# First batch of a cross-attention kernel on one core: the order of W_v·W_t, hnT's split, b_v's sums and z's first half

## The chip, the cores and the metric

The kernel runs on one core of a Trainium2 chip. The metric is the device time of one execution in microseconds (us); the median of several executions is compared.

## The reference

```python
B, C, N = (8, 256, 1024)          # x and ctx are [B, C, N], float32
def _L0_xattn_ref(x, y, w_qk, w_v, b_v, w_t, b_t):
    x_q = einsum('oc,bcn->bno', w_qk, y)
    x_k = einsum('oc,bcn->bon', w_qk, x)
    x_v = einsum('oc,bcn->bon', w_v, x) + b_v[None, :, None]
    energy = einsum('bnc,bcm->bnm', x_q, x_k)
    attention = softmax(energy, axis=-1)
    attention = attention / (1e-07 + attention.sum(axis=1, keepdims=True))
    x_r = einsum('bcn,bnm->bcm', x_v, attention)
    x_r = relu(einsum('oc,bcn->bon', w_t, x - x_r) + b_t[None, :, None])
    return x + x_r
```

The arrays that arrive hold 32 batches of this shape.

## The kernel before, in words

There is one stage ahead of everything (the set-up) and then 32 batches, of which the first is written out with orders of its own. Matmuls that need accuracy are made in three passes: each operand is split in a rounded part (hi) and a remainder (lo), and hi·hi, hi·lo and lo·hi are added up in PSUM. A "low part" is a remainder that is made by a subtraction on VectorE or GpSimd after ScalarE has made the rounded one.

The energy is y^T·G·x with G = W_qk^T·W_qk. G x is made first (four blocks of 128x512, each in a PSUM bank of its own: bank_c, bank_b, bank_a, bank_e), and then y^T·(G x) with seven products P1 to P7 of sums of blocks in place of eight. The sums of G x's blocks (T1, T2N, T4, T3) are made in the tile `ev` (also called t_raw), their parts go to gx_hi and gx_lo; the sums of y's blocks are in y_raw, y_hi and y_lo. z = x^T·(−W_v·W_t product) replaces V and the last projection: it needs hnT, the negated product of W_v and W_t, split in hnT_hi and hnT_lo.

There is no planner. Each engine has a queue of its own in the order in which the code is written, and semaphores hold an instruction until its inputs are there. An instruction that waits holds all that is behind it on its engine. The start of the first batch, in queue order:

- SyncE issues the loads: W_qk, two pieces of x, three pieces of y, W_t (L180), W_v (L181), b_v, b_t (L183, L184). The semaphore weights_in counts W_t and W_v.
- TensorE: warm-up on zeros (L869), G (L873), G·x's hi and lo·hi passes (L881, 16 matmuls of 512 columns), the pass with x's low parts (L886, 8 matmuls; each of the four blocks then counts g_done up), the product of W_v and W_t (L892, 8 matmuls of 256 columns), P1 (helper line L673, 3 matmuls), b_v's sums (L786, 8 matmuls of one column), z's first half (L736, 24 matmuls of 256 columns), P5, P6, P2, P7, P3, P4 (L673, 3 matmuls each), z's second half.
- ScalarE: the negated copy and the rounded parts of G x's blocks (L290, L291, L295, L297), y's rounded parts (L284), the rounded parts of the T sums (t_high, L303, two instructions), copies of P1's bank (L314).
- VectorE: G's split, x's low part, three sums of y, then gx_parts(0): low part of B11 (L441), T1 (L460), T2N (L464), the split of hnT (L451, L452), low part of B22 (L443), T4 (L471), low part of B21 (L443), and after it the low parts of T1 and T2N (L641, which counts t_lo_first), then bias (L644), neg_bias (L645) and eps_wb (L646).
- GpSimd: y_lo's first piece (L244), a sum of y (L246), T3 (L218, waits for T2N), y_low(0, 0) (L213), the low parts of T4 and T3 (t_low, L223), y_low for three further tiles (L213).

P1 waits for T1 (it overwrites its bank) and the low part of B11. z's first half waits for both parts of hnT. P5 waits for y_low(0, 0), for the low parts of G x's blocks and for t_lo_first, and P7 for GpSimd's t_low. ScalarE's copy of P1's bank waits for t_lo_first too, and P6 for this copy.

Of the kernel before, what the change touches and what calls it, by code (L numbers as in the profile page):

```python
# [16 lines left out]
DMA = 16  # L17
# [16 lines left out]
def xattn_kernel(nc: bass.Bass, x: bass.AP, y: bass.AP, w_qk: bass.AP, w_v: bass.AP, b_v: bass.AP,  # L34
                 w_t_T: bass.AP, b_t: bass.AP, out: bass.AP):
    B, C, N = x.shape
    KT = C // P
# [12 lines left out]
    with ctx:  # L50
# [3 lines left out]
        def sem(name):  # L54
            return ctx.enter_context(nc.semaphore(name))
# [36 lines left out]
        wv_sb = res[:, 0, KT * C:2 * KT * C].rearrange("p (k c) -> p k c", k=KT)  # L92
        wtT_sb = res[:, 1, 0:KT * C].rearrange("p (k c) -> p k c", k=KT)

        pv = ctx.enter_context(nc.psum_tensor("pv", [P, KT, N], FP32))
# [6 lines left out]
        wqk_in, weights_in, y_in = sem("wqk_in"), sem("weights_in"), sem("y_in")  # L102
# [3 lines left out]
        setup_mm, setup_dve = sem("setup_mm"), sem("setup_dve")  # L106
# [15 lines left out]
        gx_lo_done, t_made = sem("gx_lo_done"), sem("t_made")  # L122
# [305 lines left out]
        def _(dve):  # L428
            setup_steps = [0]

            def setup(ins):

                setup_steps[0] += 1
                ins.then_inc(setup_dve, 1)
                dve.wait_ge(setup_dve, setup_steps[0])

            def b_low(b, k, of, src, sign):
                dve.wait_ge(gx_hi_done, 3 * b + k + 1)
                hi = gx_hi[:, of, :].bitcast(FP32)
                if sign > 0:  # L440
                    nc.vector.tensor_tensor(gx_lo[:, of, :], src, hi, ALU.subtract).then_inc(gx_lo_done, 1)  # L441
                else:
                    nc.vector.scalar_tensor_tensor(out=gx_lo[:, of, :], in0=src, scalar=-1.0, in1=hi, op0=ALU.mult,  # L443
                                                   op1=ALU.subtract).then_inc(gx_lo_done, 1)
# [4 lines left out]
            def split_hnT():  # L449
                dve.wait_ge(setup_mm, KT + 1)  # L450
                setup(nc.vector.tensor_scalar(hnT_hi[:, :, :], h_ps, -1.0, None, ALU.mult))  # L451
                setup(nc.vector.scalar_tensor_tensor(out=hnT_lo[:, :, :], in0=h_ps, scalar=-1.0,  # L452
                                                     in1=hnT_hi[:, :, :].bitcast(FP32), op0=ALU.mult,
                                                     op1=ALU.subtract))

            def gx_parts(b, first=False):
                b_low(b, 0, B_11, row_b[:, left], 1)
                dve.wait_ge(neg_b11_made, b + 1)
                dve.wait_ge(g_done, 4 * b + 2)
                nc.vector.tensor_tensor(t_raw[:, T_1, :], row_b[:, right], neg_b11[:, :],  # L460
                                        ALU.add).then_inc(t_made, 1)
                dve.wait_ge(t_made, 3 * b + 1)
                dve.wait_ge(gx_hi_done, 3 * b + 2)
                nc.vector.tensor_tensor(t_raw[:, T_2N, :], t_raw[:, T_1, :], row_a[:, left],  # L464
                                        ALU.subtract).then_inc(t_made, 1)
                if first:
                    split_hnT()
                b_low(b, 1, B_N22, row_a[:, left], -1)
                dve.wait_ge(t_made, 3 * b + 2)
                dve.wait_ge(gx_hi_done, 3 * b + 3)  # L470
                nc.vector.scalar_tensor_tensor(out=t_raw[:, T_4, :], in0=row_a[:, right], scalar=-1.0,  # L471
                                               in1=t_raw[:, T_2N, :], op0=ALU.mult,
                                               op1=ALU.subtract).then_inc(t_made, 1)
                b_low(b, 2, B_N21, row_a[:, right], -1)
# [161 lines left out]
            nc.vector.tensor_tensor(y_raw[:, 6, :], y_raw[:, 0, :], y_raw[:, 1, :], ALU.add).then_inc(setup_y, 1)  # L636
            dve.wait_ge(setup_y, 1)
            nc.vector.tensor_tensor(y_raw[:, 5, :], y_raw[:, 4, :], y_raw[:, 1, :], ALU.add).then_inc(setup_y, 1)
            gx_parts(0, first=True)
            dve.wait_ge(t_hi_done, 1)  # L640
            nc.vector.tensor_tensor(gx_lo[:, 3:5, :], t_raw[:, 0:2, :], gx_hi[:, 3:5, :].bitcast(FP32),  # L641
                                    ALU.subtract).then_inc(t_lo_first, 1)
# [21 lines left out]
        def _(pe):  # L664
# [3 lines left out]
            def rows_of(tile):  # L668
                return slice(tile * P, (tile + 1) * P)

            def product(dst, t, ya, gb, start):
                for n, (a, g) in enumerate(((y_hi, gx_hi), (y_hi, gx_lo), (y_lo, gx_hi))):
                    last = nc.tensor.matmul(dst, a[:, ya, rows_of(t)], g[:, gb, :], start=start and n == 0,  # L673
                                            stop=n == 2, skip_group_check=not start)
                return last

            def p1(b, t, first=False):
                if first:
                    pe.wait_ge(a_lo_done, 1)
                else:  # L680
                    pe.wait_ge(y_lo_done, NP * b + t + 1)
                if t == 0:
                    pe.wait_ge(gx_lo_done, 3 * b + 1)
                    if not first:
                        pe.wait_ge(z_lo_done, 2 * b + 1)
                else:
                    pe.wait_ge(max_done, NT * b + 2 * t)
                product(bank_b, t, Y_A11, B_11, True).then_inc(b_done, 1)
# [42 lines left out]
            def z_half(par, h, first=False):  # L731
                dst = pv[:, h, :] if first else (row_b, row_a)[h][:, :]
                for i in range(NP):
                    for kt in range(KT):
                        for n, (v, w) in enumerate(((x_hi, hnT_hi), (x_hi, hnT_lo), (x_lo, hnT_hi))):
                            last = nc.tensor.matmul(dst[:, i * C:(i + 1) * C], v[par][:, kt, rows_of(h * NP + i)],  # L736
                                                    w[:, kt, :], start=(kt == 0 and n == 0),
                                                    stop=(kt == KT - 1 and n == 2))
                last.then_inc(z_done, 1)
# [38 lines left out]
                    last.then_inc(pv_done, 1)  # L778

            def very_first_pair():  # L780
                pe.wait_ge(t_made, 1)
                p1(0, 0, first=True)
                pe.wait_ge(bias_in, 2 * DMA)
                for mt in range(KT):
                    for kt in range(KT):
                        last = nc.tensor.matmul(pv[:, 1, mt:mt + 1], wtT_sb[:, kt, rows_of(mt)], bv_sb[:, kt:kt + 1],  # L786
                                                start=(kt == 0), stop=(kt == KT - 1))
                last.then_inc(setup_mm, 1)
                pe.wait_ge(setup_dve, 2)
                z_half(0, 0, first=True)  # L790
                pe.wait_ge(gx_lo_done, 3)
                pe.wait_ge(y_lo_done, 1)
                p5(0, 0, first=True)
                p6(0, 0, first=True)
                p2(0, 0)
                p7(0, 0)
                p3(0, 0).then_inc(row_a_done, 1)
                p4(0, 0)
                pe.wait_ge(setup_dve, 5)
                z_half(0, 1, first=True)  # L800
# [70 lines left out]
            for ct in range(KT):  # L871
                for kt in range(KT):
                    last = nc.tensor.matmul(pv[:, 0, ct * BANK:ct * BANK + C], wqk_sb[:, kt, rows_of(ct)],  # L873
                                            wqk_sb[:, kt, :], start=(kt == 0), stop=(kt == KT - 1))
                last.then_inc(setup_mm, 1)
            for kt in range(KT):
                pe.wait_ge(x_hi_done, kt + 1)
                for n, g in enumerate((g_hi, g_lo)):
                    pe.wait_ge(g_split, 2 * kt + n + 1)
                    for half, h, dst in g_blocks:  # L880
                        nc.tensor.matmul(dst, g[:, kt, rows_of(half)], x_hi[0][:, kt, cols_of(h)],  # L881
                                         start=(kt == 0 and n == 0), stop=False)
            pe.wait_ge(x_lo_done, KT)
            for half, h, dst in g_blocks:
                for kt in range(KT):
                    last = nc.tensor.matmul(dst, g_hi[:, kt, rows_of(half)], x_lo[0][:, kt, cols_of(h)],  # L886
                                            start=False, stop=(kt == KT - 1))
                last.then_inc(g_done, 1)
            pe.wait_ge(weights_in, 2 * DMA)
            for ct in range(KT):  # L890
                for kt in range(KT):
                    last = nc.tensor.matmul(pv[:, 0, KT * C + ct * C:KT * C + (ct + 1) * C], wv_sb[:, kt, rows_of(ct)],  # L892
                                            wtT_sb[:, kt, :], start=(kt == 0), stop=(kt == KT - 1))
            last.then_inc(setup_mm, 1)
            run_batches(pe, lambda b: batch(b, 0, first=True), lambda b: batch(b, 1), batch,
                        lambda b: batch(b, 1, last=True))
            w_block(1, 1, 1, apart=bank_c, of=(1,)).then_inc(w_apart, 1)
# [25 lines left out]
```

## Time and profile before

| | |
|---|---|
| median of 3 runs | 1847.72 us (1847.33 to 1847.95) |
| the profiled execution | 1848.28 us |
| its span | 1846.4 us |
| TensorE matmul busy | 1840.8 us |
| VectorE, ScalarE, GpSimd busy | 1500.6, 1310.2, 787.4 us |
| granted TensorE clock, whole span | 1.0 |

The span is the time from the first to the last instruction of the profiled execution; what lies around it is 1.88 us. Busy time is that of instructions at work, and a matmul's end is modelled, so a busy TensorE may still hold short pauses; the weight loads (PEld) show these better.

### The profile page before, as it was taken

What the parts mean: (1) busy time and instruction counts of PE and PEld (TensorE: products, weight loads), DVE (VectorE), ACT (ScalarE), POOL (GpSimd) and SP (SyncE); (2) the same over time, 40 slices, a digit from 0 to 9 for tenths busy, and PEclk for the clock granted to TensorE, in tenths of its full rate; (3) what the DMA queues carried; (4) which work ended last, traced back from release to release, by engine and by line L of the source; (5) the groups of instructions that cost most, each with busy time, mean ns of one, the idle gap of its engine ahead of it and who ended that gap; (6) DMA issues with size and microseconds to landing.
All of it is one profiled execution on the core that took longest, in us unless ns stands there. A gap on an engine that the chain in (4) does not pass through costs nothing.

```text
span 1846.4 us, 26426 instructions
## 1 busy us (share of the span) xinstructions
PE 1840.8 (100%) x8895; PEld 1552.8 (84%) x8895; DVE 1500.6 (81%) x2034; ACT 1310.2 (71%) x1798; POOL 787.4 (43%) x421
## 2 busy tenths in 40 slices
PE   9999999999999999999999999999999999999999
PEld 8888888888888888888888888888888888888887
DVE  7878787787887877878878788788787877878878
ACT  7767776677666786667776677766677666776665
POOL 5543344432444424444244452344533444334431
PEclk9999999999999999999999999999999999999999
DMA  3201112011220211101112111211011120111201
GB/s 108 69 24 56 60 68 68 23 68 46 68 68 23 68 46 68 68 33 58 46 68 68 49 42 46 68 68 62 29 50 64 68 68 23 64 50 69 69 1 46
DMA packets 34090, 101.92 MB, mean 55 GB/s; under 512 B 4224, under 2 KB 5248, under 8 KB 34048
## 3 DMA queue, kind: packets, MB, share of 16 engines
q1 hardware_dynamic: 33760, 101.07, 15.9%
q10 hardware_dynamic: 288, 0.39, 0.1%
q8 instruction: 13, 0.21, 0.1%
q14 instruction: 29, 0.24, 0.0%
HBM read 67.90 MB, written 33.55 MB: 55 GB/s over the span
## 4 chain that ended last, share of the span: by engine, by line
PE 99%; ACT 0%; DVE 0%; issue 0%; DVEq 0%; POOL 0%; ACTq 0%; POOLq 0%
PE pv L773 37%; PE row_b L673 19%; PE row_a L673 14%; PE pv L745 9%; PE row_b L736 5%; PE row_a L736 5%; PE row_a L727 5%; PE row_b L727 5%; PE pv L736 0%; PE pv L869 0%; DVE colsum L513 0%; PE pv L873 0%; PE pv L855 0%; PE row_a L881 0%; PE row_b L881 0%; ACT y_hi L284 0%
## 5 line engine op out<-in xcount | busy, mean ns | idle before, releaser
L213 POOL TENSOR_TENSOR y_lo<-y_raw,y_hi 128x896 fp32r<-128x896 f32 (+1 forms) x128 | 277.4, 2189 | 545.0 <-ACT y_hi L284 355.4
L520 DVE SCALAR_TENSOR_TENSOR p_lo<-p_sb,row_inv,p_hi 128x1024 fp32r<-128x1024 f32 x254 | 325.3, 1282 | 96.3 <-ACT p_hi L331 96.1
L314 ACT ACTIVATE ev<-row_b 128x512 f32<-128x512 f32 x384 | 229.3, 597 | 199.8 <-PE row_b L673 199.1
L198 POOL TENSOR_TENSOR x_lo<-x_sb,x_hi 128x1024 fp32r<-128x1024 f32 x63 | 152.3, 2417 | 448.9 <-ACT x_hi L272 448.9
L323 ACT ACTIVATE p_sb<-p_sb,neg_max 128x1024 f32<-128x1024 f32 x256 | 295.2, 1154 | 28.5 <-DVE neg_max L495 24.6
L331 ACT ACTIVATE p_hi<-p_sb,row_inv 128x1024 fp32r<-128x1024 f32 x256 | 292.5, 1143 | 30.9 <-PE pv L773 30.1
L513 DVE SCALAR_TENSOR_TENSOR colsum<-p_sb,row_inv,colsum 128x1024 f32<-128x1024 f32 x224 | 292.4, 1306 | 8.5 <-DVE row_inv L503 0.6
L773 PE MATMUL pv<-p_hi,z_hi 128*128 128x512 f32 x1024 | 273.7, 389 | 0.0
L773 PE MATMUL pv<-p_hi,z_lo 128*128 128x512 f32 x1024 | 273.7, 389 | 0.0
L495 DVE CUSTOM_DVE_ANT_0 p_sb<-row_a,ev 128x1024 f32<-128x1024 f32 x128 | 156.5, 1223 | 142.5 <-PE row_a L673 142.5
L773 PE MATMUL pv<-p_lo,z_hi 128*128 128x512 f32 (+1 forms) x1047 | 271.7, 383 | 0.0
L773 PEld LDWEIGHTS pv<-p_lo,z_hi 128*128 128x128 f32 x1047 | 196.5, 188 | 40.8
L773 PEld LDWEIGHTS pv<-p_hi,z_hi 128*128 128x128 f32 x1024 | 192.2, 188 | 39.9
L773 PEld LDWEIGHTS pv<-p_hi,z_lo 128*128 128x128 f32 x1024 | 192.2, 188 | 39.9
L673 PE MATMUL row_b<-gx_hi,y_hi 128*128 128x512 f32 x512 | 199.6, 390 | 0.1
L673 PE MATMUL row_b<-gx_lo,y_hi 128*128 128x512 f32 x512 | 199.4, 390 | 0.0
L673 PE MATMUL row_b<-gx_hi,y_lo 128*128 128x512 f32 x512 | 199.4, 390 | 0.0
L495 DVE CUSTOM_DVE_ANT_0 p_sb<-row_b,ev 128x1024 f32<-128x1024 f32 x128 | 156.6, 1223 | 11.1 <-PE row_b L673 11.1
L223 POOL TENSOR_TENSOR gx_lo<-ev,gx_hi 128x1024 fp32r<-128x1024 f32 x63 | 150.7, 2415 | 1.3 <-ACT gx_hi L303 1.3
L673 PE MATMUL row_a<-gx_hi,y_hi 128*128 128x512 f32 x384 | 149.8, 390 | 0.3
L673 PE MATMUL row_a<-gx_lo,y_hi 128*128 128x512 f32 x384 | 149.6, 390 | 0.0
L673 PE MATMUL row_a<-gx_hi,y_lo 128*128 128x512 f32 x384 | 149.5, 389 | 0.0
(142 smaller groups left out, 3581.2 us busy)
## 6 DMA issues: line engine op xcount, KB each, us to landing
x_sb<-x SPq DMA_DIRECT2D x64, 512.0 KB, 4.5
out<-res SPq DMA_DIRECT2D x62, 512.0 KB, 3.3
y_raw<-y SPq DMA_DIRECT2D x64, 256.0 KB, 3.8
y_raw<-y SPq DMA_DIRECT2D x32, 512.0 KB, 3.8
out<-res SPq DMA_DIRECT2D x2, 256.0 KB, 2.2
res<-w_qk SPq DMA_DIRECT2D x1, 256.0 KB, 2.9
res<-w_t_T SPq DMA_DIRECT2D x1, 256.0 KB, 7.4
res<-w_v SPq DMA_DIRECT2D x1, 256.0 KB, 7.8
```

Source lines behind the costliest of these rows:

```text
L213: nc.gpsimd.tensor_tensor(y_lo[:, of:, cols], y_raw[:, 1 + of:8, cols], y_hi[:, of:, cols].bitcast(FP32), ALU.subtract).then_inc(y_lo_done, 1)
L314: nc.scalar.activation(ev[:, to, :], bank_b, ACT.Copy, scale=scale).then_inc(b_copied, 1)
L323: nc.scalar.activation(p_sb[r][:, :], p_sb[r][:, :], ACT.Exp, scale=-1.0, bias=neg_max[:, j:j + 1], accum_out=row_sum[:, j:j + 1]).then_in ...
L331: nc.scalar.activation(p_hi[r][:, :], p_sb[r][:, :], ACT.Copy, scale=row_inv[:, j:j + 1]).then_inc(p_hi_done, 1)
L495: nc.vector.tensor_tensor_reduce(out=p_sb[r][:, :], in0=(row_a, row_b)[r][:, :], in1=ev[:, 2 * r:2 * r + 2, :].rearrange("p k n -> p (k n) ...
L513: nc.vector.scalar_tensor_tensor(out=colsum[:, :], in0=p_sb[r][:, :], scalar=inv, in1=colsum[:, :], op0=ALU.mult, op1=ALU.add).then_inc(ac ...
L520: nc.vector.scalar_tensor_tensor(out=p_lo[r][:, :], in0=p_sb[r][:, :], scalar=row_inv[:, j:j + 1], in1=p_hi[r][:, :].bitcast(FP32), op0=AL ...
L673: last = nc.tensor.matmul(dst, a[:, ya, rows_of(t)], g[:, gb, :], start=start and n == 0, stop=n == 2, skip_group_check=not start)
L727: last = nc.tensor.matmul(dst, g[:, kt, rows_of(half)], v[par][:, kt, cols_of(h)], start=(kt == 0 and n == 0), stop=(kt == KT - 1 and n == 2))
L736: last = nc.tensor.matmul(dst[:, i * C:(i + 1) * C], v[par][:, kt, rows_of(h * NP + i)], w[:, kt, :], start=(kt == 0 and n == 0), stop=(kt ...
L745: last = nc.tensor.matmul(to, w[:, kt, rows_of(mt)], v[par][:, kt, cols_of(h)], start=(apart is not None and kt + n == 0), stop=(kt == KT ...
L773: last = nc.tensor.matmul(pv[:, mt, cols], z[:, j, rows_of(mt)], p[r][:, cols], start=(t + r + n == 0), stop=(t == NP - 1 and r == 1 and n ...
```

## The change

TensorE makes the product of W_v and W_t between L881 and L886, so ahead of the pass of G x with x's low parts. VectorE splits hnT ahead of the first gx_parts, where it stood between T2N and the low part of B22. In the first pair of batch 0, TensorE does b_v's sums and z's first half ahead of P1, where P1 stood first. All instructions and their sizes are the same; three orders change. Batches 1 to 31 have the same code.

```diff
-            def gx_parts(b, first=False):
+            def gx_parts(b):
...
-                if first:
-                    split_hnT()
                 b_low(b, 1, B_N22, row_a[:, left], -1)
...
-            gx_parts(0, first=True)
+            split_hnT()
+            gx_parts(0)
...
             def very_first_pair():
-                pe.wait_ge(t_made, 1)
-                p1(0, 0, first=True)
                 pe.wait_ge(bias_in, 2 * DMA)
...
                 pe.wait_ge(setup_dve, 2)
                 z_half(0, 0, first=True)
+                pe.wait_ge(t_made, 1)
+                p1(0, 0, first=True)
                 pe.wait_ge(gx_lo_done, 3)
...
+            pe.wait_ge(weights_in, 2 * DMA)
+            for ct in range(KT):
+                for kt in range(KT):
+                    last = nc.tensor.matmul(pv[:, 0, KT * C + ct * C:KT * C + (ct + 1) * C], wv_sb[:, kt, rows_of(ct)],
+                                            wtT_sb[:, kt, :], start=(kt == 0), stop=(kt == KT - 1))
+            last.then_inc(setup_mm, 1)
             pe.wait_ge(x_lo_done, KT)
...
                 last.then_inc(g_done, 1)
-            pe.wait_ge(weights_in, 2 * DMA)
-            for ct in range(KT):
-                for kt in range(KT):
-                    last = nc.tensor.matmul(pv[:, 0, KT * C + ct * C:KT * C + (ct + 1) * C], wv_sb[:, kt, rows_of(ct)],
-                                            wtT_sb[:, kt, :], start=(kt == 0), stop=(kt == KT - 1))
-            last.then_inc(setup_mm, 1)
```

## Rows read from the trace of the kernel before

**Rows 1.** The page: TensorE's busy time, and the chain that ended last by engine.

```profile
PE 1840.8 (100%) x8895; PEld 1552.8 (84%) x8895; DVE 1500.6 (81%) x2034; ACT 1310.2 (71%) x1798; POOL 787.4 (43%) x421
...
PE 99%; ACT 0%; DVE 0%; issue 0%; DVEq 0%; POOL 0%; ACTq 0%; POOLq 0%
```

**Rows 2.** Waits of the weight loads, whole span: us in total, times, longest.

```profile
PEld row_b L673 <- POOL gx_lo L223: 0.5, 1, 0.5
```

**Rows 3.** The chain in order of time, 0 to 32 us: start, us, what.

```profile
12.35 0.91 PE row_a L886 x4
13.26 1.73 PE pv L892 x8
...
15.68 0.79 PE pv L786 x8
16.50 3.01 PE pv L736 x24
```

**Rows 4.** Timeline and DMA issues (us from issue to landing), and traffic by stretch.

```profile
4.12 0.92 SPq L181 DMA_DIRECT2D res<-w_v  x1
...
res<-w_v SPq DMA_DIRECT2D x1, 256.0 KB, 7.8
...
11.20:11.30 0.10, 0.10 (x3) 0.06 (x2) 0.10 (x2) 0.00 (x0) 0.00 (x0) 1.00 0.24 82
```

**Rows 5.** Timeline, TensorE: the pass after L881, and P5.

```profile
11.29 1.07 PE L886 MATMUL row_b<-x_lo,g_hi 128*128 128x512 f32 x4
...
19.64 0.47 PE L673 MATMUL row_a<-gx_hi,y_hi 128*128 128x512 f32 x1
19.95 0.39 PE L673 MATMUL row_a<-gx_lo,y_hi 128*128 128x512 f32 x1
```

**Rows 6.** Timeline, VectorE: start, us, instruction.

```profile
13.06 0.69 DVE L441 TENSOR_TENSOR gx_lo<-row_b,gx_hi 128x512 fp32r<-128x512 f32 x1 [0.63 <-ACT gx_hi L291]
...
14.38 0.69 DVE L464 TENSOR_TENSOR ev<-ev,row_a 128x512 f32<-128x512 f32 x1
15.03 0.69 DVE L451 TENSOR_SCALAR hnT_hi<-pv 128x512 fp32r<-128x512 f32 x1
...
16.48 0.69 DVE L443 SCALAR_TENSOR_TENSOR gx_lo<-row_a,gx_hi 128x512 fp32r<-128x512 f32 x1
...
18.28 1.21 DVE L641 TENSOR_TENSOR gx_lo<-ev,gx_hi 128x1024 fp32r<-128x1024 f32 x1
```

**Rows 7.** Timeline, ScalarE.

```profile
11.94 0.60 ACT L290 ACTIVATE neg_b<-row_b 128x512 f32<-128x512 f32 x1 [0.88 <-PE row_b L886]
...
15.38 1.04 ACT L303 ACTIVATE gx_hi<-ev 128x1024 fp32r<-128x1024 f32 x1
16.33 0.93 ACT L284 ACTIVATE y_hi<-y_raw 128x896 fp32r<-128x896 f32 x1
17.80 1.06 ACT L303 ACTIVATE gx_hi<-ev 128x1024 fp32r<-128x1024 f32 x1 [0.53 <-DVE ev L471]
```

**Rows 8.** Timeline, GpSimd.

```profile
15.15 1.28 POOL L218 TENSOR_TENSOR ev<-neg_b,ev 128x512 f32<-128x512 f32 x1 [0.34 <-DVE ev L464]
16.40 1.28 POOL L213 TENSOR_TENSOR y_lo<-y_raw,y_hi 128x512 fp32r<-128x512 f32 x1
19.00 2.74 POOL L223 TENSOR_TENSOR gx_lo<-ev,gx_hi 128x1024 fp32r<-128x1024 f32 x1 [1.32 <-ACT gx_hi L303]
```

**Rows 9.** Timeline later in batch 0: GpSimd, then VectorE's column sums.

```profile
46.46 2.41 POOL L198 TENSOR_TENSOR x_lo<-x_sb,x_hi 128x1024 fp32r<-128x1024 f32 x1
...
46.49 3.46 DVE L513 SCALAR_TENSOR_TENSOR colsum<-p_sb,row_inv,colsum 128x1024 f32<-128x1024 f32 x1
...
50.06 1.28 DVE L513 SCALAR_TENSOR_TENSOR colsum<-p_sb,row_inv,colsum 128x1024 f32<-128x1024 f32 x1
```

**Rows 10.** The tile res, 0 to 30 us: matmuls' duration in ns, min/median/max, first and last start.

```profile
L873 PE MATMUL pv<-res x8: 379/634/634, 4.7 to 7.4; 128*128 128x256 f32 x8
...
L892 PE MATMUL pv<-res x8: 377/379/379, 13.1 to 14.6; 128*128 128x256 f32 x8
```

## The prediction

> **What bounds the kernel now.** I read the page first. TensorE is busy for 1840.8 us of a span of 1846.4 us, and 99% of the chain that ended last is TensorE [rows 1]. So a change of order can only give back or add pauses of TensorE. Next I read what the weight loads waited for, because a pause that the modelled end of a matmul hides is seen there. In the whole span only a handful of waits is left, all in the first 30 us or in the last batch; the one that bears on this change is 0.5 us for GpSimd's low parts ahead of P7 [rows 2]. So what is lost or won in the first 22 us is neither absorbed nor multiplied later: it goes into the time one to one, and the question is how much later or earlier P5 and P7 start. Then I read the chain in order of time and the timeline of each engine up to P5.
>
> In this stretch TensorE isn't all of the story. VectorE works without a pause from the low part of B11 (13.06) to the end of L641 (18.28 + 1.21 = 19.49), and P5 follows at 19.64 [rows 5, 6]. P7 comes after GpSimd's L223, which ends at 19.00 + 2.74 = 21.74 [rows 8]. So VectorE's queue sets P5, and what starts that queue is the first block of G x by way of ScalarE: L290 at 11.94, L441 1.12 us later [rows 6, 7].
>
> **The change part by part.**
>
> *The wait for the weights.* The product of W_v and W_t waits for both transfers. W_v was issued at 4.12 and landed 7.8 us later, at 11.92; data still moved at 11.2 to 11.3 (82 GB/s) [rows 4]. Before, the product came at 13.26 in the chain [rows 3] and this cost nothing. Now it stands where L886 stood, whose first matmul ran at 11.29 [rows 5]. It can start at about 11.98: 0.7 us of pause, and 0.1 us more because a matmul after a wait is longer (0.47 us for P5's first and 0.39 us for its second [rows 5]). I take 0.8 us. The bounds are 0.1 us (all landed at 11.3, when the traffic fades) and 1.1 us (landing 0.3 us later in other runs; that is my allowance). Queued behind this wait are L886, all four blocks of G x and so ScalarE's L290 and VectorE's gx_parts.
>
> *The product ahead of L886.* Its eight matmuls take 1.73 us in the chain [rows 3]. All four blocks of G x come 0.8 + 1.73 = 2.53 us later. L290 goes from 11.94 to 14.47, L441 from 13.06 to 15.59.
>
> *The split of hnT.* It takes 16.48 − 15.03 = 1.45 us of VectorE's queue [rows 6]. The product was ready at 13.26 + 1.73 = 14.99; it now is at 14.99 − 1.82 (L886's eight matmuls, 0.91 us for each four [rows 3]) + 0.8 = 13.97. The split runs from 14.03 to 15.48, in the hole that VectorE has before 15.59, so it costs nothing, with 0.11 us to spare. This takes 1.45 us out of the path between T2N and L641.
>
> *VectorE up to L641.* L464 starts 1.32 us after L441, at 16.91, and ends at 17.60. L443 follows at once (0.65 us, as L451 did), and from L443 to L641 it is 18.28 − 16.48 = 1.80 us [rows 6]. L641 is so due at 19.36 and not 18.28: 2.53 − 1.45 = 1.08 us later. The product and its wait cost more than the split gives back.
>
> *GpSimd against L641.* T3 on GpSimd waits for T2N: from 17.68 for 1.28 us; y_low(0, 0) follows after 1.25 us, 18.93 to 20.21 [rows 8]. Before, y_low had ended at 17.68 and L641 began at 18.28, because the split lay between. Now L641 is due at 19.36, in the middle of y_low. What that does is seen later in the batch: a column sum that normally takes 1.28 us was begun 0.03 us after a GpSimd subtraction of 2.41 us and took 3.46 us, to 49.95, which is 1.08 us after GpSimd had ended at 48.87 [rows 9]. The two took turns. L641 also reads two tiles of SBUF, so I let it run after y_low: 20.21 + (1.21 − 0.20) = 21.22, against 19.49 before: 1.73 us later. The bounds are 19.36 + 1.21 = 20.57 (no turn-taking, 1.08 us later) and 21.42 (all of its 1.21 us after GpSimd). I take 21.22, from the row nearest in kind.
>
> Here the Trainium skill is weighed against the trace: the page "SBUF — State Buffer", section "Who interferes with whom", says that a VectorE instruction with two SBUF inputs and a GpSimd instruction that reads SBUF exclude each other, and that whoever comes first holds the port to its end. The column sum above agrees (1.08 us behind GpSimd's end), and no row shows it for a TENSOR_TENSOR that comes second. By the rule L641 is held and the sum is 1.73; without it the sum is some 1.3.
>
> *b_v's sums, z's first half, P1.* L886 is done at 13.97 + 1.82 = 15.79. Then 0.79 us for L786 and up to 3.01 us for z's first half [rows 3], to at most 19.6; hnT's parts are there at 15.44, so z doesn't wait. P1 is three matmuls at 0.91/4 = 0.23, 0.69 us, to 20.3; T1 and the low part of B11 have long been made. P5 waits for L641 until 21.22 + 0.15 = 21.37. TensorE's work is no bound here, and moving P1 behind z costs and gives nothing: ScalarE's copy of P1 waits for L641 as well. The cover is 1.1 us; without it P1 would add its 0.69 us.
>
> *P7.* ScalarE's first L303 needs T2N: 17.64, then L284 0.95 us later and the second L303 another 0.85 us on, 19.44 to 20.50 [rows 7]. GpSimd's L223 is then free to start at 20.64, but L641 runs to 21.22. Before, L641 ended at 19.49 and L223 2.25 us after it; now 21.22 + 2.25 = 23.47, against 21.74: 1.73 us later. P7 keeps its distance to P5, and the 0.5 us wait of rows 2 stays.
>
> *Sum.* +0.80 (weights) + 1.73 (product) − 1.45 (split) + 0.65 (L641 behind y_low: 21.22 − 20.57) = +1.73 us. From P5 on every order is the same and every engine is shifted alike. Span 1846.4 + 1.7 = 1848.1 us, the profiled execution 1848.28 + 1.7 = 1850.0 us. It lay 0.56 us over the median of the runs, so the median becomes 1847.72 + 1.7 = 1849.4 us, 0.09% slower. What a measurement of this kernel can tell from no change is about 0.2%, 3.7 us.
>
> **The rivals.**
>
> *L641 isn't held by GpSimd.* For it: in rows 9 it is another instruction. Against it: the same kind of operands. P5 would come at +1.08. L223 would start at 20.64 and take between 2.25 and 2.74 us, to 22.9 to 23.4, and P7 with it: about +1.3 us, 1849.0 us.
>
> *The weights are there in time.* The data of W_v faded at about 11.3 us; if the wait costs at most 0.1 us, everything is 0.7 us less: +1.0 us, 1848.7 us. Against it is the landing at 11.92.
>
> *The change gives what it could at best.* If product and wait together cost G x less than the split's 1.45 us, P5 comes earlier, down to where TensorE has no pause: 0.14 us ahead of P5 and some 0.2 us ahead of P7 would go, −0.35 us, 1847.4 us. For that the product would have to take under 1.45 us without any wait; it takes 1.73 us.
>
> *The clock falls, slower by over 0.2%.* TensorE now has two pauses, about 0.7 us ahead of the product and about 1 us ahead of P5. In the first 7 us a matmul of the product's shape takes 634 ns, later 379 ns [rows 10], so TensorE starts at the lower of its two levels (1.2 GHz, then 2.4 GHz), though the page's granted clock is 1.0 in every stretch. That start lasted from about 1.1 to 6.9 us. If a pause threw it back, a stretch as long, 5.8 us at half speed, would cost 2.9 us on top: +4.6 us, 1852.3 us. It decides if one of the pauses is enough. Against it: pauses of 0.5 us left the level as it was, and the work on both sides of each is dense. The Trainium skill, page "TensorE: Matmul & The Clock Gate", section "HAM oscillation — how this bites in real kernels", tells of such falls behind waits for DMA that are longer than these; no row here shows one.
>
> **How the numbers follow.** Forecast (weights late, L641 held) 0.62; L641 not held 0.14; weights in time 0.11; at best 0.04; clock 0.04; something else, mostly of the size of the first cases, 0.05. The first cases span +1.0 to +2.1 us (the upper end with 1.1 us of wait and 0.2 us more for L641); with the runs' own scatter of 0.3 us each way and the best case taken in this makes 1847.4 to 1850.7, and I go to 1851.2 because the landing of one transfer was seen once only. Within 0.2% is then 0.95, slower 0.04, faster 0.01: no case reaches −3.7 us.
>
> **What would show each step.** The first weight load of L892 near 11.9 to 12.0 us with a wait on a DMA ahead of it; L290 near 14.5; L451 near 14.0 and L441 near 15.6; L641 with a duration of about 1.9 us, ending near 21.2, and GpSimd's y_low under it near 18.9; P5 near 21.4 after a pause of 1 us; P7 near 23.8; no other gap between the two kernels behind it. It would be wrong if L892 didn't wait, if L641 took 1.21 us in spite of GpSimd, or if matmuls of 512 columns behind the pauses took longer than 0.39 us.

## The result, and the profile after

The changed kernel takes 1849.97 us (median of 22 runs, 1849.33 to 1850.96), the kernel before 1847.93 us beside it (22 runs). The ratio is 1.0012 with a 95% interval of 1.0006 to 1.0017: slower by 2.0 us, clear of the scatter but well under 0.2%. The prediction was 1849.4 us and within 0.2%. The profiled execution has a span of 1848.2 us and a time of 1850.12 us.

First the waits of the weight loads in the changed kernel, the view of [rows 2] (us in total, times, longest):

```profile
PEld row_a L672 <- issue: 1.8, 1, 1.8
PEld pv L885 <- DMA res<-w_v: 1.7, 1, 1.7
...
PEld row_b L880 <- ACT x_hi L272: 0.7, 1, 0.7
PEld row_b L672 <- POOL gx_lo L223: 0.5, 1, 0.5
```

Two pauses come from the change, both in the first 22 us: the product of W_v and W_t (L885, was L892) waits for W_v, and P5 (L672, was L673) waits 1.8 us. The 0.7 us at L880 is a wait for the rounded part of x ahead of everything that was moved; profiles of other versions have it or not, as x's second piece lands. The 0.5 us ahead of P7 is the old one. Then the DMA issues (us from issue to landing) and TensorE's timeline with the three places, the view of [rows 4, 5]:

```profile
res<-w_v SPq DMA_DIRECT2D x1, 256.0 KB, 8.2
...
12.31 1.99 PE L885 MATMUL pv<-res 128*128 128x256 f32 x8 [1.24 <-DMA res<-w_v]
...
21.87 0.47 PE L672 MATMUL row_a<-gx_hi,y_hi 128*128 128x512 f32 x1 [1.40 <-DVE gx_lo L640]
...
24.28 0.47 PE L672 MATMUL row_b<-gx_hi,y_hi 128*128 128x512 f32 x1
```

W_v landed at 4.12 + 8.2 = 12.3 us and the product began at once. P5 begins at 21.87 (before 19.64), P7 at 24.28 (before 22.05): 2.23 us later.

What sets P7 is not GpSimd's L223, though the view of the waits names it. P7 also waits for ScalarE's copy of P6's bank (the second L314; `b_copied` in `p7`). Its row and P7's first weight load, in the kernel before and then in the changed one:

```profile
21.30 0.60 ACT L314 ACTIVATE ev<-row_b 128x512 f32<-128x512 f32 x1 [0.66 <-PE row_b L673]
22.02 0.19 PEld L673 LDWEIGHTS row_b<-gx_hi,y_hi 128*128 128x128 f32 x1 [0.49 <-POOL gx_lo L223]
...
23.54 0.60 ACT L314 ACTIVATE ev<-row_b 128x512 f32<-128x512 f32 x1 [0.66 <-PE row_b L672]
24.25 0.19 PEld L672 LDWEIGHTS row_b<-gx_hi,y_hi 128*128 128x128 f32 x1 [0.49 <-POOL gx_lo L223]
```

The copy ends at 21.90 and 24.14, and P7's weights follow 0.12 and 0.11 us later; L223 had ended at 21.74 and 23.98, 0.28 and 0.27 us ahead of them. The copy follows P6 and P6 follows P5, so the distance from P5 to P7 is a matter of this chain.

Now VectorE, ScalarE's first copy and GpSimd, the views of [rows 6 to 8]:

```profile
14.35 0.69 DVE L451 TENSOR_SCALAR hnT_hi<-pv 128x512 fp32r<-128x512 f32 x1 [1.47 <-PE pv L885]
15.07 0.69 DVE L452 SCALAR_TENSOR_TENSOR hnT_lo<-pv,hnT_hi 128x512 fp32r<-128x512 f32 x1
16.00 0.69 DVE L441 TENSOR_TENSOR gx_lo<-row_b,gx_hi 128x512 fp32r<-128x512 f32 x1 [0.24 <-ACT gx_hi L291]
...
17.32 0.69 DVE L464 TENSOR_TENSOR ev<-ev,row_a 128x512 f32<-128x512 f32 x1
17.93 0.68 DVE L443 SCALAR_TENSOR_TENSOR gx_lo<-row_a,gx_hi 128x512 fp32r<-128x512 f32 x1
...
19.73 2.00 DVE L640 TENSOR_TENSOR gx_lo<-ev,gx_hi 128x1024 fp32r<-128x1024 f32 x1
...
14.80 0.60 ACT L290 ACTIVATE neg_b<-row_b 128x512 f32<-128x512 f32 x1 [3.30 <-PE row_b L891]
...
19.35 1.30 POOL L213 TENSOR_TENSOR y_lo<-y_raw,y_hi 128x512 fp32r<-128x512 f32 x1
21.04 2.94 POOL L223 TENSOR_TENSOR gx_lo<-ev,gx_hi 128x1024 fp32r<-128x1024 f32 x1 [0.39 <-ACT gx_hi L303]
```

The reader is to see four things. The split of hnT (L451, L452) lies in a hole of VectorE ahead of L441. ScalarE's first copy is 2.86 us later than in [rows 7]. From L443 at 17.93 there is no split in the queue any more, so L640 (was L641) is due 4.93 us after L290, where it was due 6.34 us after it. And L640 takes 2.00 us where it took 1.21: it was begun at 19.73 while GpSimd's y_low ran from 19.35 to 20.65, and ended 1.08 us after y_low did.

The later start stays. At 64 us the changed kernel is 2.16 us behind (the run of P·V matmuls that starts at 66.21 started at 64.05 before), and the last instruction of VectorE is 1.83 us behind. Between these two marks no new wait is named. The distance from the one to the other is 1778.36 us in before, 1778.36 in a second profile of the changed kernel and 1778.03 in the first, so 0.3 us of it is scatter between executions.

### The profile page after: what moved, and what is told of

Same layout as the page of the kernel before. It is cut to its first block, busy times and chain, and to the rows that moved or that the text cites. A ratio compares the mean times of both kernels' runs of the same rounds, so it can differ in the third digit from the quotient of the medians.

```text
span 1848.2 us, 26426 instructions
## 1 busy us (share of the span) xinstructions
PE 1839.9 (100%) x8895; PEld 1551.8 (84%) x8895; DVE 1501.5 (81%) x2034; ACT 1310.4 (71%) x1798; POOL 787.2 (43%) x421
## 4 chain that ended last, share of the span: by engine, by line
PE 98%; DVE 0%; ACT 0%; DMA 0%; SPq 0%; issue 0%; DVEq 0%; ACTq 0%
PE pv L772 37%; PE row_b L672 19%; PE row_a L672 14%; PE pv L744 9%; PE row_b L735 5%; PE row_a L726 5%; PE row_a L735 5%; PE row_b L726 5%; DMA res<-w_v 0%; DVE colsum L511 0%; PE pv L735 0%; PE pv L885 0%; DVE gx_lo L640 0%; PE pv L854 0%; ACT y_hi L284 0%
## 5 line engine op out<-in xcount | busy, mean ns | idle before, releaser
L314 ACT ACTIVATE ev<-row_b 128x512 f32<-128x512 f32 x384 | 229.3, 597 | 199.5 <-PE row_b L672 198.5
L198 POOL TENSOR_TENSOR x_lo<-x_sb,x_hi 128x1024 fp32r<-128x1024 f32 x63 | 152.1, 2414 | 449.1 <-ACT x_hi L272 449.1
L672 PE MATMUL row_b<-gx_hi,y_hi 128*128 128x512 f32 x512 | 199.6, 390 | 0.1
L672 PE MATMUL row_b<-gx_lo,y_hi 128*128 128x512 f32 x512 | 199.5, 390 | 0.0
L672 PE MATMUL row_b<-gx_hi,y_lo 128*128 128x512 f32 x512 | 199.5, 390 | 0.0
L672 PE MATMUL row_a<-gx_hi,y_hi 128*128 128x512 f32 x384 | 149.9, 390 | 1.6 <-DVE gx_lo L640 1.4
L223 POOL TENSOR_TENSOR gx_lo<-ev,gx_hi 128x1024 fp32r<-128x1024 f32 x63 | 150.8, 2415 | 0.4 <-ACT gx_hi L303 0.4
L672 PE MATMUL row_a<-gx_lo,y_hi 128*128 128x512 f32 x384 | 149.6, 390 | 0.0
L672 PE MATMUL row_a<-gx_hi,y_lo 128*128 128x512 f32 x384 | 149.5, 389 | 0.0
```

The source lines that it names most:

```text
L314: nc.scalar.activation(ev[:, to, :], bank_b, ACT.Copy, scale=scale).then_inc(b_copied, 1)
```

## The experiments

Each kernel was timed in five rounds beside the kernel before, whose median was 1848.22 us in the first group of four, 1847.98 in the second and 1847.99 in the third. "Over before" is the difference of these medians. The uncertainty of one ratio is about 0.0009, or 1.7 us. Most of the differences below are smaller than that, so a median is evidence here only together with its profile. Between profiles, places are compared by their distance from ScalarE's L290, since the time of L290 itself scatters from one execution to the next.

**The changed kernel again** (no edit).

> The changed kernel once more, beside which the next three are read. Theory A (the weights come too late for the product's new place, and L640 is held by GpSimd's y_low): the first weight load of L885 waits for the transfer of W_v, which lands between 11.9 and 12.3 us; L640 takes about 2.0 us; P5 starts 21.4 to 21.9 us, P7 23.8 to 24.3 us; median 1.5 to 2.2 us over the kernel before. A rival (the 2 us are scatter between chips) expects a difference under 1 us here.

1850.63 us, 2.4 us over before, ratio 1.0014 (1.0005 to 1.0023). The wait for W_v was 1.3 us here, L640 took 2.01 us, P5 began at 21.32. The cost is there again, 0.2 us above what I had expected. In this profile P5 was 0.1 us earlier than expected, as W_v landed at 11.6 us.

**Without the wait for the weights.**

```diff
-            pe.wait_ge(weights_in, 2 * DMA)
...
-                    last = nc.tensor.matmul(..., wv_sb[:, kt, rows_of(ct)], wtT_sb[:, kt, :], ...)
+                    last = nc.tensor.matmul(..., wqk_sb[:, kt, rows_of(ct)], wqk_sb[:, kt, :], ...)
...
             def very_first_pair():
+                pe.wait_ge(weights_in, 2 * DMA)
```

> The changed kernel with W_qk, which has long landed, in both operands of the product of L885, so that it needn't wait for W_v and W_t (they are waited for ahead of b_v's sums); the output is another one. Theory A: no wait of L885 on a DMA, its first weight load at 10.6 to 11.1 us, everything up to P7 1.0 to 1.6 us earlier than in the changed kernel: P5 20.3 to 20.9 us, span 1846.8 to 1847.2 us, still 0.4 to 1.0 us over before. Rival B (the wait is hidden, the order of the queues alone costs the 2 us): P5 and the span stay within 0.3 us of the changed kernel's.

1849.12 us, 0.9 us over before (ratio 1.0007, 0.9998 to 1.0016) and 1.5 us under the changed kernel's second group of runs (a 95% range of 0.7 to 1.9 by the scatter of the executions). Its profile, the weight loads and TensorE's timeline:

```profile
9.88 1.71 PEld L885 LDWEIGHTS pv<-res 128*128 128x128 f32 x8
...
19.57 0.47 PE L672 MATMUL row_a<-gx_hi,y_hi 128*128 128x512 f32 x1 [1.33 <-DVE gx_lo L640]
```

The product starts at 9.88 with no wait, earlier than I had thought TensorE could be there. P5 is 0.7 us earlier than the earliest that I had expected. The wait is on the path, and by the medians it costs nearer 1.5 us than the 0.8 us of the prediction (1.1 us if the main result's 2.0 us is compared). Rival B falls.

**Without GpSimd's y_low(0, 0).**

```diff
-            y_low(0, 0, sums=True)
+            pool.wait_ge(y_hi_done, 1)
+            nc.gpsimd.memset(y_lo[:, 3:, 0:P].bitcast(FP32), 0.0).then_inc(y_lo_done, 1)
```

> The changed kernel with GpSimd's y_low(0, 0) replaced by filling that part of y_lo with zeros, which reads nothing and is short; this low part is left out of the result. Theory A: L640 takes 1.2 us in place of 2.0 us and P5 comes 0.8 us earlier, 20.7 to 21.2 us; P7 only about 0.5 us earlier, because GpSimd's L223 then waits for ScalarE's second L303; span 0.4 to 0.6 us less than the changed kernel's. Rival C (L640 is long for a reason of its own or ScalarE's): it stays at 2.0 us and nothing moves.

1850.09 us, 1.9 us over before and 0.5 us under the changed kernel, which the medians alone can't tell from nothing. VectorE, GpSimd and P5 in its timeline (the lines moved by one):

```profile
19.68 1.22 DVE L641 TENSOR_TENSOR gx_lo<-ev,gx_hi 128x1024 fp32r<-128x1024 f32 x1
...
19.30 0.53 POOL L249 MEMSET y_lo<- 128x512 f32 x1
21.00 2.43 POOL L223 TENSOR_TENSOR gx_lo<-ev,gx_hi 128x1024 fp32r<-128x1024 f32 x1 [1.18 <-ACT gx_hi L304]
...
21.05 0.47 PE L673 MATMUL row_a<-gx_hi,y_hi 128*128 128x512 f32 x1 [0.61 <-DVE gx_lo L641]
...
23.48 0.50 PE L673 MATMUL row_b<-gx_hi,y_hi 128*128 128x512 f32 x1
```

With no subtraction on GpSimd, VectorE's instruction is back at 1.22 us and P5 comes 0.8 us earlier. GpSimd's L223 drops from 2.94 to 2.43 us too, as nothing on VectorE is in its way, but it starts no earlier, since it waits for ScalarE. P7 comes at 23.48, 0.8 us earlier as well and not 0.5 as expected: in the changed kernel it was ScalarE's copy that held it, and the copy moves with P5. Here L223 (to 23.43) is what P7 waits for. Part of the 0.8 us is lost again behind it. The weight loads wait longer for ScalarE's copies near 41, 51 and 53 us (0.40, 0.21 and 0.66 us; in the changed kernel 0.20, none and 0.52), and the P·V matmuls of 66.21 start at 65.86, 0.35 us earlier. Rival C falls.

**Both of these.** (Both diffs above.)

> Both edits together. Theory A: the two add up, 1.5 to 2.1 us less than the changed kernel, so within 0.5 us of the kernel before (what is left is the product's 1.73 us less the split's 1.45 us, and ScalarE's queue ahead of P7): P5 near 19.5 to 20.2 us. If another cost hides under these two, the kernel stays 1 us or more over before.

1848.78 us, 0.6 us over before (1.0003, 0.9994 to 1.0012), 1.85 us under the changed kernel. The single gains were 1.5 and 0.5 us, so they add up within the scatter, and what is left is about what the product less the split should leave. The distances from L290 in its profile agree: P7 is 8.73 us behind it (10.11 before), and the P·V matmuls that started at 64.05 before are 50.92 us behind it (52.11 before). Against the product's 1.73 us this is 1.38 us given back at P7 and 1.19 us near 65 us. The time of this profiled execution is not one to read the size from: the second piece of x landed late in it, and TensorE waited 2.0 us for it ahead of all this (P5 at 20.97).

**The product back behind the x pass.** The six lines of the product stand behind the L891 loop again, as before the change; the rest is the changed kernel.

> The changed kernel with the product of W_v and W_t back behind the pass with x's low parts; the split stays ahead of gx_parts, z ahead of P1. Theory A (VectorE's queue from the first block of G x on is the path, and the split must have its input in time): ScalarE's first copy L290 near 11.9 us again, but the split runs 15.0 to 16.5 us and holds the low part of B11 until 16.5 (before 13.06); L640's instruction ends near 22.1 us, P5 about 22.3 us, 10.3 us after L290; the kernel is 2.2 to 3.0 us over before, so slower than the changed one. Rival (the product's place alone costs the time): back at the time of before within 0.5 us.

1851.15 us, 3.2 us over before, ratio 1.0019 (1.0010 to 1.0028). ScalarE's L290 starts at 11.16 in its profile, and VectorE's queue waits for the product:

```profile
14.25 0.69 DVE L451 TENSOR_SCALAR hnT_hi<-pv 128x512 fp32r<-128x512 f32 x1 [2.14 <-PE pv L891]
...
15.70 0.69 DVE L441 TENSOR_TENSOR gx_lo<-row_b,gx_hi 128x512 fp32r<-128x512 f32 x1
...
21.56 0.47 PE L672 MATMUL row_a<-gx_hi,y_hi 128*128 128x512 f32 x1 [2.04 <-DVE gx_lo L640]
...
22.86 0.63 PE L672 MATMUL row_b<-gx_hi,y_lo 128*128 128x512 f32 x1
23.29 0.63 PE L672 MATMUL row_a<-gx_hi,y_hi 128*128 128x512 f32 x1
```

The median lies 0.2 us above the range that I had expected. P5 comes 10.4 us after L290 (10.3 expected). The split ahead of gx_parts is only free if the product is early. The last two lines are new: from 1.1 us behind the end of the pause of 2.5 us a matmul of 512 columns takes 0.63 us and not 0.39. The windows of this profile (the number before the last two is the granted clock) say why:

```profile
23.00:24.00 1.00, 1.00 (x4) 0.81 (x3) 0.84 (x2) 0.47 (x1) 1.00 (x2) 0.50 0.00 0
24.00:25.00 1.00, 1.00 (x4) 0.67 (x4) 0.00 (x0) 1.00 (x3) 1.00 (x1) 0.50 0.00 0
```

The granted clock is 0.50, the lower of TensorE's two levels (1.2 GHz), from about 22.7 to 26.1 us. This is the rival that I had given 0.04, in a sibling of the changed kernel. 7 of the 11 executions have a mean clock of 0.999 and a median of 1851.76 us, the other 4 have 1.0 and 1850.92 us. Of the 33 executions of the kernel before beside them none is below 1.0 (3 of 33 and 3 of 31 in the other two groups).

**The split back in its old place.** `split_hnT()` stands between T2N and the low part of B22 again; the product stays early.

> The changed kernel with hnT's split back between T2N and the low part of B22; the product stays early, z stays ahead of P1. Theory A: 1.45 us come back in VectorE's queue; L640's instruction no longer meets y_low and takes 1.2 us; z then starts late and P1 behind it sets P5: 0.7 to 1.0 us more than the changed kernel at P5 and P7, so 2.7 to 3.1 us over before in the median. Rival (the split's place is of no account): same as the changed kernel.

1852.06 us, 4.1 us over before, ratio 1.0024 (1.0015 to 1.0033). L641 took 1.22 us, as said. The waits of the weight loads:

```profile
PEld pv L736 <- DVE hnT_lo L452: 2.5, 1, 2.5
...
PEld row_b L673 <- ACT ev L314: 0.5, 1, 0.5
```

P5 begins at 22.40, 8.05 us after L290, where the changed kernel has 7.07: +0.98 us, as expected. P7 comes 10.70 us behind L290 where the changed kernel has 9.48: +1.22 us, more than the 0.7 to 1.0 expected. The median missed the expectation by 1 us. The 5 executions with a mean clock of 1.0 have 1851.4 us, 3.4 over before; the 6 below it 1852.7 us. So the mechanism held up to P5. What I had left out is that P6 waits 0.5 us for ScalarE's copy of P1, which now ends late, and, by the medians, the clock. The profiled execution shows no fall itself: its granted clock is 1.00 throughout the first 50 us, in spite of the pause of 2.5 us.

**P1 first again.** The two lines of P1 stand ahead of b_v's sums again; product and split as changed.

> The changed kernel with P1 back ahead of b_v's sums and z. Theory A (TensorE's work isn't the bound there): TensorE waits for T1 about 1 us, then P1, the sums and z end just when L640's does; P5 the same or up to 0.3 us later than in the changed kernel, the median within 0.4 us of it. Rival (moving P1 behind z is what costs): about the time of before.

1850.54 us, 2.6 us over before. The 9 executions at a clock of 1.0 have 1850.35 us, 2.4 over before: the same as the changed kernel. The profiled one is one of the other two. Its waits and TensorE's timeline:

```profile
PEld row_b L672 <- DVE ev L460: 1.6, 1, 1.6
...
20.13 0.41 PE L735 MATMUL pv<-hnT_hi,x_hi 128*128 128x256 f32 x1
```

P1 waits 1.6 us for T1; then z's matmuls take 0.41 us in place of 0.28, from 19.0 to 22.4 us, with the granted clock at 0.50. It fell 2.1 us behind the end of that pause; 0.8 us of waiting for W_v and 1.0 us for the rounded part of x lie further ahead. By the medians P1's place does not matter to the changed kernel as long as the clock holds.

**Only P1 moved, in the kernel before.** `p1(0, 0, first=True)` and its wait stand behind z's first half; product and split as before.

> The kernel before with only P1 moved behind z's first half. Theory A: P1 leaves a pause of TensorE that it filled (while hnT is split) and adds its 0.69 us behind z, where before had 0.3 us of waiting: P5 0.3 to 0.4 us later than in before (near 20.0 us), P7 0.2 to 0.4 us later; median 0.2 to 0.5 us over before. Rival (P1's place costs 1 us or more): P5 beyond 20.6 us.

1848.65 us, 0.7 us over before (1.0003, 0.9994 to 1.0013). The waits of its weight loads:

```profile
PEld pv L736 <- DVE hnT_lo L452: 0.8, 1, 0.8
PEld row_b L673 <- ACT ev L314: 0.5, 1, 0.5
```

The median is 0.2 us above what I had expected. P5 comes 8.1 us after L290 (7.7 before), as expected. P7 comes 10.8 us after it and not 10.1: P1 ends at 20.0 us, so ScalarE's copy of its bank is no longer ready when P6 needs it. In the changed kernel this is hidden, because L640 ends later than P1.

**The pauses filled.** In the kernel with the product back, matmuls on zeros go into the two pauses (3 ahead of z, 8 behind P1), into PSUM that is free then.

> The product_back kernel with matmuls on zeros in its two pauses: three ahead of z (of some 0.8 us) and eight behind P1 (of some 2.5 us), written to a part of PSUM that is free then; they end before what is waited for. Theory D (in 7 of 11 executions of product_back the granted clock fell to 0.5 for some 3 us behind these pauses, which costs about 0.8 to 1.4 us where it happens, and it is the pauses that do it): a mean clock of 1.0 in at least 10 of 11 executions, the median 0.3 to 0.9 us under product_back's, near 2.5 us over before. Rival (the falls come from elsewhere): as many executions at 0.999 as without the fill, and the same median.

1852.45 us (9 executions), worse than without the fill by 1.3 us. I had mis-sized it:

```profile
20.39 3.61 PE L793 MATMUL pv<-zeros 128*128 128x256 f32 x16
```

The 8 matmuls are 16 in the trace, 3.4 us and not 1.7, and P5 waits for them (23.65, when L640 ended at 22.1). The time says nothing for the theory then. The clock does: only 1 of 9 executions is below a mean of 1.0, against 7 of 11, and their times lie within 0.9 us (2.7 us without the fill). The one below 1.0 is no slower than the rest.

**y_low ahead of T3.** A real version; all work is done.

```diff
-            t_three(0)
             y_low(0, 0, sums=True)
+            t_three(0)
```

> The changed kernel with GpSimd's y_low(0, 0) ahead of T3, so that GpSimd is free of it when L640 is due; all work is done. Theory A: L640 is held only by T3's end, takes 1.3 to 1.6 us in place of 2.0, P5 comes about 0.6 us earlier relative to ScalarE's L290 (6.4 us behind it, not 7.07), P7 about 0.35 us earlier because T3 is later; median 0.2 to 0.6 us under the changed kernel's, still 1.3 us or more over before.

1850.28 us, 2.3 us over before. The timeline of VectorE:

```profile
19.98 1.38 DVE L640 TENSOR_TENSOR gx_lo<-ev,gx_hi 128x1024 fp32r<-128x1024 f32 x1
```

L640 takes 1.38 us, P5 comes 6.45 us after L290 (6.4 expected, 7.07 in the changed kernel) and P7 8.97 us (9.48). So 0.5 us is given back in the profile. Against the changed kernel's 2.0 and 2.4 us over before, the median doesn't show it: inconclusive in time.

**The weights loaded ahead of y.** The two loads of L180 and L181 stand ahead of y's three.

> The changed kernel with the loads of W_t and W_v issued ahead of y's three. Theory A: the product no longer waits (first weight load of L885 10.5 to 11.1 us), but y now lands near 12 us, its sums fill VectorE until 13.9 us and the split comes behind them: L441 near 15.3 us in place of 15.6 to 16.0; median 0.2 to 0.8 us under the changed kernel's, not under before. If y's lateness costs more than the wait did, it is over the changed kernel.

1850.97 us, 3.0 us over before: the expectation missed. The weight loads, VectorE, and a window of 5 us:

```profile
10.73 1.71 PEld L885 LDWEIGHTS pv<-res 128*128 128x128 f32 x8
...
11.89 0.69 DVE L633 TENSOR_TENSOR y_raw<-y_raw 128x512 f32<-128x512 f32 x1 [1.68 <-DMA y_raw<-y]
...
20.00:25.00 5.00, 4.00 (x11) 3.18 (x12) 3.25 (x4) 2.91 (x6) 4.82 (x2) 0.68 0.00 0
```

The product waits for nothing and L441 comes at 15.15, as I had said, and P5 at 21.00. But the pause is now one of 2.3 us ahead of P5, and 8 of 11 executions have a mean clock below 1.0: their median is 1851.07 us, that of the other three 1849.30 us. The order of the loads gave the wait back, and the clock took more than that.

**The rounded part of hnT on ScalarE, in the kernel before.** ScalarE makes hnT_hi behind its fourth copy of G x; VectorE makes only hnT_lo, behind the low part of B22.

> The kernel before with the rounded part of hnT made by ScalarE, which waits 0.8 us there, in place of VectorE, and the low part of hnT behind the low part of B22: takes 0.7 us out of VectorE's queue, which sets P5. Expected: L641 due near 17.6 us instead of 18.28, P5 near 19.3 us (then TensorE's own work is the bound), P7 0.3 to 0.4 us earlier; the median 0.2 to 0.5 us under before at best, which is at the edge of what 11 runs can tell. If ScalarE's queue becomes the path, no gain or a loss up to 0.5 us.

1847.73 us, 0.3 us under before, ratio 0.9999 (0.9990 to 1.0008). ScalarE's row and P5:

```profile
15.08 0.60 ACT L413 ACTIVATE hnT_hi<-pv 128x512 fp32r<-128x512 f32 x1 [1.02 <-PE pv L895]
...
19.37 0.39 PE L676 MATMUL row_a<-gx_hi,y_hi 128*128 128x512 f32 x1
```

P5 comes 7.4 us after L290 and follows z without a pause; P7 9.7 us after it, 0.4 us less than before. It is the one version whose profile is ahead of both kernels, by an amount that these runs can't tell from nothing.

## Why the prediction was right, by its own steps

*What bounds it.* That nothing in the first 22 us is absorbed later held to within 0.2 us: 2.23 us at P7, 2.16 at 64 us, 2.0 in the median. By pieces it was less exact, as the next steps show: in versions with one pause taken out, up to 0.5 us of what P7 gained was lost again by 65 us.

*The wait for the weights, 0.8 us.* Right in kind, too small. It was priced by one execution of before, in which TensorE reached the place at 11.06 us. It was there late: its start-up matmuls were slow until 6.9 us ([rows 10]: median 634 ns), while in the changed kernel's profile the median of the same eight is 380 ns, and TensorE was at the place at 10.64 us although it had waited 0.7 us for x. Without the wait the product began at 9.88. And W_v landed at 12.3, not 11.9. In six profiles of kernels with this wait it lasted 0.8 to 2.0 us. By the medians it costs 1.1 to 1.5 us. It only costs that much because TensorE could have used the time. The kernel before has such early arrivals too: in the profiles that keep its order there, the first matmul behind L881 comes between 10.5 and 11.3 us, and the profile that I read has one of the latest.

*The product, 1.73 us, less the split, 1.45 us.* Right. From L290 to L640 the changed kernel is 1.41 us shorter (forecast 1.45). With wait and y_low both taken out 0.6 us is left of the 2.4 us, where the sum of the prediction leaves 0.28 us. In that version's profile 0.35 us of the product's 1.73 is left at P7 and 0.54 us near 65 us, as TensorE waits 0.3 us for ScalarE's copy near 41 us. Two kernels show that the pair belongs together: with the product back, 3.2 us over before, with the split back, 4.1.

*L640 behind y_low, 0.65 us.* Right: the rows have it at 1.98 to 2.01 us wherever y_low runs under it and at 1.21 to 1.22 where nothing does. Its end, 1.08 us after GpSimd's, is the 1.08 us of [rows 9]; the forecast took 1.01 us, so it came 0.07 us late. VectorE's x_lo (L630, else 1.23 us) shows the same in one profile (P1 first again): begun at 8.77 under GpSimd's L198 (to 9.97 us), it took 2.28 us and ended 1.08 us after it. The price is 0.8 us at P5 and P7 and some 0.5 us in the kernel, because TensorE then waits longer for ScalarE's copies in the next pairs. By the Trainium skill, page "SBUF — State Buffer", section "Who interferes with whom", a VectorE instruction with two SBUF inputs and a reading GpSimd instruction exclude each other; here the trace agrees for a TENSOR_TENSOR as well (2.00 us with the subtraction under it, 1.22 without).

*P1 behind z costs nothing, cover 1.1 us.* Right for the changed kernel (P1 first again: the same at a clock of 1.0). What I said of the cover's end was short: without it not only P1's matmuls but also ScalarE's copy of its bank come late (0.7 us in the kernel before, where I had expected 0.2 to 0.5).

*P7 keeps its distance to P5.* The distance is right, 2.41 us in both, but not the reason. I had P7 wait for GpSimd's L223, with 2.25 us from the end of L641 to the end of L223. L223 does end 2.25 us after L640, but it is the copy of P6's bank that is last, in both kernels. P5 and P7 moved alike because the chain from P5 over P6 and the copy is the same. With L223 as the bound, taking out y_low could give P7 only 0.5 us, and it gave 0.8. That the wrong path gave the right number here was luck.

*The sum.* 1.73 us was forecast and 2.0 us measured. The wait was priced 0.3 to 0.7 us too low, the product less the split 0.3 us too low, and the hold 0.1 to 0.2 us too high in what it costs the kernel. The medians' scatter is as large as the rest, so the sum is not confirmed to the last 0.3 us.

*The rivals.* L641 not held: no. Weights in time: no. At best: no, and the version without wait and without y_low is the nearest to it. The clock: it did not fall in the changed kernel's profile, and 2 of its 33 executions have a mean below 1.0, no slower than the rest, so it isn't in the result. But it was a nearer miss than 0.04 says: of the siblings with 2.3 to 2.5 us of pause ahead of P5 or z, 21 of 33 executions have a mean clock below 1.0. The price that I gave it, 2.9 us, was too high; the stretch at the lower level lasts some 3.4 us in each of the three profiles that have it, which at half speed is an estimated 1.7 us, and the medians show 0.8 to 1.8 us.

What stays open: why the same pause costs the clock in one execution and not in the next (of the three profiles with such a pause, two show the fall). That the fall comes from the pause is supported by the filled kernel, whose clock held, but that kernel also began everything else later, so it isn't shown apart from that.

## What to carry to other kernels

To move work forward past a wait for a transfer, price the wait by the earliest time at which the engine can be there in any execution, not by the one in the profile. When a queue of VectorE gets shorter, look at what GpSimd does at the new time: a subtraction that had lain in the gap can now lie under the next one. A pause of TensorE can cost more than itself: behind pauses of 2.3 and 2.5 us the work ran at half the clock for 3.4 us in two of three profiles here. And where a view names one engine for a wait, look at when each of the awaited instructions ended: GpSimd's had been done for 0.27 us, and ScalarE's copy was last.

## What the runs showed of the hardware that I had not expected

The clock falls behind pauses as short as these, and not at once. Behind a pause of 2.5 us and one of 2.3 us the granted clock went to 0.50 for about 3.4 us and matmuls of 512 columns from 0.39 to 0.63 us; in the version with P1 first it fell behind waits of 1.0, 0.8 and 1.6 us. In each, TensorE had been at work again for 0.9 to 2.1 us when it fell. In the changed kernel, with waits of 0.7, 1.7 and 1.8 us, it held. The mean clock of an execution is only a hint: it can be 0.999 because of the idle end alone, as in the profiled execution without the wait (a single window below 1.00, from 1800 us), and then nothing is lost.

A tiny VectorE instruction can be held as long as a big one. L644 (L645 before), 128x2 values from SBUF to SBUF, takes 2.2 us wherever GpSimd's L223 has begun before it (it ends within 0.03 us of L223's end), and 0.17 us in the kernels in which it began first or in the same hundredth of a us.

A matmul of the program on float32 operands is two rows of the trace, some 0.21 us apart at 256 columns, so a fill of 8 was 16. The product of W_v and W_t, four matmuls in the code, is the 8 rows of L892 for the same reason.
